# Cutting GpSimd's two runs of 16 products into pieces of four heads, with small mask products and a new order of the third stage

## The reference

```python
# L1_attn (letter D): 16 heads of 16 channels, 4 key heads, rope, a sink per head
att = einsum('bhqd,bhkd->bhqk', q, k) * hd ** (-0.5) + sink
att = softmax(where(band, att, -inf));  out = einsum('bhqk,bhkd->bqhd', att, v) @ wo
# L1_xattn (letter E): inside one token, 16 heads against 16 heads
Q, K, V = (x @ Wq.T + bq), (ctx @ Wk.T + bk), (ctx @ Wv.T + bv)   # as (token, 16, 16)
weight = softmax(einsum('bshd,bsgd->bshg', Q, K))
out = einsum('bshg,bsgd->bshd', weight, V) @ Wo.T + bo
# L1_ffn (letters F, M): causal attention, whose output goes only into a rank-16 modulation
mod = 0.1 * tanh(attn @ A)
gate = silu(h @ W_in.T + mod * (h @ A) @ B);  out = residual + gate * (h @ W_up.T) @ W_down.T
```

## Time and profile before

| | us |
|---|---|
| median of 3 runs | 3019.28 (3017.0 to 3025.15) |
| the profiled execution | 3016.38, span 3014.7 |
| first query product of the first tile | 1983.1 |
| last query product of the last tile | 2925.1 |

### The profile page before, as it was taken

One profiled execution on the slowest core, in us unless ns is written; L12 is line 12 of the kernel. 1 busy time (PEld: TensorE's weight loads), 2 busy tenths in 40 slices (PEclk: granted clock), 3 DMA queues, 4 the chain that ended last, 5 costly groups with the idle time before them and its releaser, 6 DMA issues. The chain is left out here.

```text
span 3014.7 us, 68300 instructions
## 1 busy us (share of the span) xinstructions
PE 2755.2 (91%) x22096; PEld 2297.8 (76%) x22128; DVE 2487.1 (83%) x5468; ACT 1990.4 (66%) x4233; POOL 2099.5 (70%) x2618
## 2 busy tenths in 40 slices
PE   6999999999999999999799499667899999999988
PEld 3888888888888888888555399535777777777767
DVE  6888888888888888888599677468889898989873
ACT  5888878878787887878576355345566666666642
POOL 6897666666666666666467544379898988898870
PEclk9999999999999999999899699768999999999999
DMA  4555444444434444444344499500000000000000
GB/s 145 176 197 167 134 138 139 146 139 131 143 132 141 139 146 140 132 153 132 116 155 158 173 333 341 191 15 19 20 24 23 24 22 24 22 24 23 21 4 11
DMA packets 185883, 340.11 MB, mean 113 GB/s; under 512 B 40668, under 2 KB 104037, under 8 KB 178936
## 3 DMA queue, kind: packets, MB, share of 16 engines
q1 hardware_dynamic: 179448, 319.55, 32.1%
q0 software_dynamic: 6144, 16.79, 1.7%
HBM read 264.68 MB, written 63.19 MB: 109 GB/s over the span
## 5 line engine op out<-in xcount | busy, mean ns | idle before, releaser
L1843 POOL TENSOR_TENSOR l_prod<-l_sco,l_kv 128x256 f32<-128x256 f32 x512 | 370.1, 762 | 35.4 <-DVE l_sco L2350 35.4
L1836 POOL TENSOR_TENSOR l_prod<-l_q,l_kv 128x256 f32<-128x256 f32 x512 | 359.2, 741 | 45.7 <-DVE l_att L2358 45.7
L718 DVE SCALAR_TENSOR_TENSOR a_cq<-a_PQ,a_taps,a_cq 128x504 f32<-128x504 f32 (+2 forms) x384 | 281.9, 734 | 74.9 <-ACT a_cq L584 65.8
L718 DVE SCALAR_TENSOR_TENSOR a_ck<-a_PK,a_taps,a_ck 128x504 f32<-128x504 f32 (+2 forms) x384 | 280.8, 731 | 9.4 <-ACT a_ck L584 0.3
L342 POOL TENSOR_TENSOR a_tq<-a_cq,a_tq 128x512 f32<-128x512 f32 x128 | 166.0, 1297 | 130.7 <-ACT a_tq L590 130.3
L329 POOL TENSOR_TENSOR a_hrs<-a_hve,a_neghalf 128x8 f32<-128x8 f32 x128 | 209.7, 1638 | 25.3 <-DVE a_hve L735 25.3
L485 PE MATMUL a_Y<-a_wo,a_og_parts 128*128 128x256 f32 x1536 | 207.2, 285 | 4.5 <-POOL a_og_parts L336 4.5
L412 PEld LDWEIGHTS a_X<-a_wv,a_xb 128*128 128x128 f32 x1536 | 199.8, 188 | 12.1 <-issue 1.2
L412 PE MATMUL a_PQ<-a_x_hi,a_wqk 128*128 (+1 forms) x512 | 196.1, 424 | 12.6 <-issue 11.9
L342 POOL TENSOR_TENSOR a_tk<-a_ck,a_tk 128x512 f32<-128x512 f32 x128 | 163.6, 1278 | 62.8 <-ACT a_tk L590 62.8
L412 PE MATMUL a_X<-a_wv,a_xb 128*128 128x256 f32 x1536 | 204.1, 282 | 0.8 <-DMA a_xb<-a_x_lo 0.8
(11 more groups left out here) (403 smaller groups left out, 8412.4 us busy)
## 6 DMA issues: line engine op xcount, KB each, us to landing
a_wqk<-qk_parts SPq DMA_DIRECT2D x112, 512.0 KB, 3.3
m_wgu<-gate_up_parts SPq DMA_DIRECT2D x39, 1024.0 KB, 7.9
a_wv<-v_parts SPq DMA_DIRECT2D x56, 512.0 KB, 3.7
a_wg<-g_parts SPq DMA_DIRECT2D x112, 256.0 KB, 3.1
a_wo<-o_parts SPq DMA_DIRECT2D x112, 256.0 KB, 2.8
a_dr<-decays SPq DMA_DIRECT2D x256, 64.0 KB, 2.5
m_hs<-sorted_rows SPq DMA_DIRECT2D x39, 256.0 KB, 7.1
sorted_outs<-m_ys SPq DMA_DIRECT2D x39, 256.0 KB, 7.3
```

The costliest lines, as they stand in the source:

```text
L718: nc.vector.scalar_tensor_tensor(out=acc, in0=src, scalar=taps[p][:, tap + k:tap + k + 1], in1=acc, op0=ALU.mult, op1=ALU.add).then_inc(s_ ...
L1836: nc.gpsimd.tensor_tensor(out=prod[:, h], in0=qv[:, h:h + 1, :].to_broadcast([P, H, HD]), in1=kk, op=ALU.mult).then_inc(S("E_pqk"), 1)
L1843: nc.gpsimd.tensor_tensor(out=prod[:, h], in0=sco[:, h:h + 1, :].to_broadcast([P, HD, H]), in1=vv, op=ALU.mult).then_inc(S("E_pav"), 1)
```

## The change

It has five parts.

1. GpSimd's products are cut into pieces of four heads. `q` and `sco` exist twice. Within an iteration, the first four heads of the next tile's queries come ahead of this tile's values; the values go in the order heads 4 to 15, then 0 to 3; heads 4 to 15 of the next tile's queries follow. Each piece waits for its own group of `prod`. VectorE's list follows: the scores of group 0 belong to the next tile, and the values of group 0 come last.
2. The gathers read the row numbers in `slots` directly; `of_tile` and the tiny instructions go.
3. The mask and sink products become four products of 64x512 each, one for each quarter of the array (`rows` by `s`).
4. `ft_gm` writes its result back into PSUM (`MI`), and `ft_gm_hi` and `ft_gm_lo` read it there.
5. The lists of all engines have a new order.

```diff
-        kv, q = [sb(f"kv{k}", [P, 2, D]) for k in range(3)], sb("q", [P, D])
+        kv, q = [sb(f"kv{k}", [P, 2, D]) for k in range(3)], [sb(f"q{k}", [P, D]) for k in range(2)]
-        sco, se = sb("sco", [P, H, H]), sb("se", [P, 3, H])
+        sco, se = [sb(f"sco{k}", [P, H, H]) for k in range(2)], sb("se", [P, 3, H])
...
-            def products_qk(t):
-                pool.wait_ge(S("E_q"), t + 1)
-                wait_if(pool, S("E_att"), 4 * t)
-                for h in range(H):
+            def products_qk(part):
+                def piece(t):
+                    pool.wait_ge(S("E_q"), t + 1)
+                    for h in range(4 * part, 4 * part + 4):
+                        if part == 0 and h == 0 and t >= 2:
+                            pool.wait_ge(S("E_att"), 4 * t - 4)
+                        if part and t and h % 4 == 0:
+                            pool.wait_ge(S("E_att"), 4 * t - 4 + h // 4)
...
+            def products_av(part):
+                def piece(t):
+                    pool.wait_ge(S("E_w"), t + 1)
+                    if part == 0:
+                        pool.wait_ge(S("E_sc0"), min(t + 2, TILES))
...
-                nc.gpsimd.tensor_copy(of_tile[:], slots[:, tile(t), :].rearrange("p t k -> p (t k)")).then_inc(S("G_at"), 1)
...
-                for half in range(2):
-                    if k == "F":
-                        nc.tensor.matmul(SS[:, half, :], identb[:], cmask[:], start=True, stop=False, skip_group_check=True)
-                    else:
-                        nc.tensor.matmul(SS[:, half, :], inverse3[:], sink3[:, half, :], start=True, stop=False, skip_group_check=True)
+                for s in range(2):
+                    for half in range(2):
+                        out = SS[s * SEQ:(s + 1) * SEQ, half, :]
+                        if k == "F":
+                            rows = slice(half * SEQ, (half + 1) * SEQ)
+                            nc.tensor.matmul(out, identb[rows, rows], cmask[rows], start=True, stop=False, skip_group_check=True)
+                        else:
+                            rows = slice(half * SEQ, half * SEQ + 3)
+                            nc.tensor.matmul(out, inverse3[rows], sink3[rows], start=True, stop=False, skip_group_check=True)
...
-                nc.vector.tensor_tensor(out=part[64:64 + R, :], in0=gmT[:], in1=part[0:R, :].bitcast(F32), op=ALU.subtract).then_inc(S("F_gm3"), 1)
+                nc.vector.tensor_tensor(out=part[64:64 + R, :], in0=MI[0:R, P:2 * P], in1=part[0:R, :].bitcast(F32), op=ALU.subtract).then_inc(S("F_gm3"), 1)
...
-            iterate(pool, [("F", power("F", 2)), ("Et", products_av), ("Dn", power("D", 1)), ("En", power("E", 1)), ("E", products_qk),
+            iterate(pool, [("F", power("F", 2)), ("E", products_qk(0)), ("Et", products_av(1)), ("Et", products_av(2)), ("Et", products_av(3)),
```

More of the change, by code:

```diff
@@ L1839, in products_av @@
[L1839 to L1849, removed]
-                nc.gpsimd.tensor_copy(of_tile[:], slots[:, tile(t), :].rearrange("p t k -> p (t k)")).then_inc(S("G_at"), 1)
[L1851 to L1854, removed]
+            def products_qk(part):
+                def piece(t):
+                    pool.wait_ge(S("E_q"), t + 1)
+                    pool.wait_ge(S(f"kv_in{t % 3}"), 16 * (t // 3 + 1))
+                    qv = q[t % 2][:].rearrange("p (h d) -> p h d", d=HD)
+                    kk = kv[t % 3][:, 0, :].rearrange("p (g d) -> p g d", d=HD)
+                    for h in range(4 * part, 4 * part + 4):
[3 more added lines that the diff above has]
+                            pool.wait_ge(S("E_att"), 4 * t - 4 + h // 4)
+                        nc.gpsimd.tensor_tensor(out=prod[:, h], in0=qv[:, h:h + 1, :].to_broadcast([P, H, HD]), in1=kk,
+                                                op=ALU.mult).then_inc(S("E_pqk1" if part else "E_pqk0"), 1)
+                return piece
@@ new lines, in products_av @@
+            def products_av(part):
[3 more added lines that the diff above has]
+                        pool.wait_ge(S("E_sc0"), min(t + 2, TILES))
+                    vv = kv[t % 3][:, 1, :].rearrange("p (d g) -> p d g", d=HD)
+                    for h in range(4 * part, 4 * part + 4):
+                        nc.gpsimd.tensor_tensor(out=prod[:, h], in0=sco[t % 2][:, h:h + 1, :].to_broadcast([P, HD, H]), in1=vv,
+                                                op=ALU.mult).then_inc(S("E_pav"), 1)
+                return piece
@@ L1855, in gather, with piece @@
+            def gather(k):
+                def piece(t):
+                    if t:
+                        pool.wait_ge(S("G_x"), 2 * t - 1 + k)
                     nc.gpsimd.indirect_dma_start(got[k][:], None, outs[:, :],
-                                                 bass.IndirectOffsetOnAxis(ap=of_tile[:, k:k + 1], axis=0)).then_inc(S(f"G_in{k}"), 16)
+                                                 bass.IndirectOffsetOnAxis(ap=slots[:, t, k:k + 1], axis=0)).then_inc(S(f"G_in{k}"), 16)
+                return piece
@@ L1858, in _ @@
             pool.wait_ge(S("masked"), 4)
-            iterate(pool, [("F", power("F", 2)), ("Et", products_av), ("Dn", power("D", 1)), ("En", power("E", 1)), ("E", products_qk),
-                           ("G", gather)])
+            iterate(pool, [("F", power("F", 2)), ("E", products_qk(0)), ("Et", products_av(1)), ("Et", products_av(2)), ("Et", products_av(3)),
+                           ("Et", products_av(0)), ("E", products_qk(1)), ("E", products_qk(2)), ("Dn", power("D", 1)), ("En", power("E", 1)),
+                           ("E", products_qk(3)), ("G", gather(0)), ("G", gather(1))])
@@ L2116, in e_q @@
             def e_q(t):
-                wait_if(act, S("E_pqk"), H * t)
+                if t >= 2:
+                    act.wait_ge(S("E_pqk1"), 12 * (t - 1))
                 act.wait_ge(S("E_qp"), t + 1)
-                nc.scalar.activation(q[:], EB[:, 0:D], ACT.Copy).then_inc(S("E_q"), 1)
+                nc.scalar.activation(q[t % 2][:], EB[:, 0:D], ACT.Copy).then_inc(S("E_q"), 1)
             def exponentials(k):
@@ L2222, in et_exp @@
                 act.wait_ge(S("E_sub"), t + 1)
-                nc.scalar.activation(sco[:], sco[:], ACT.Exp).then_inc(S("E_exp"), 1)
+                nc.scalar.activation(sco[t % 2][:], sco[t % 2][:], ACT.Exp).then_inc(S("E_exp"), 1)
             def split_high(t):
```

85 lines of the change are left out of this document (40 added, 45 removed).

## The result

The changed kernel takes 3122.23 us (median of 4 runs, 3097.49 to 3125.05) against 3018.14 for the kernel before: 1.0335 times as long, interval 1.0282 to 1.0388. It is slower; 2979 was forecast, and the range ended at 3014. The profiled execution is its quickest run, 3097.49, with a span of 3095.6 against 3014.7 before.

A forecast was written before the change was run, and what follows sets the result against it. TensorE, VectorE and GpSimd were all taken as nearly full. Iterations fall from 30.02 to 28.7 us: 36 us over 27, plus 4 in the ramp, so 2979 us on the runs' median; range 2953 to 3014.

The forecast's parts named there:

- VectorE (b): VectorE's cost of new overlap with GpSimd: weights 0.3 us, shift and low part of F 0.2 together, per iteration.
- GpSimd's stop for the last value sum: GpSimd's 1.25 us wait per iteration for VectorE's last value sum, from sharing `prod`; forecast to go.
- Small products: TensorE's four mask or sink products run side by side, 0.33 us instead of 0.53, saving 0.2 per stage.
- The 0.62: TensorE's 0.62 us wait before the output product, for ScalarE's copy of the transposed result; forecast to stay.
- all three engines were within two microseconds of full: TensorE, VectorE and GpSimd nearly full per iteration, so removing GpSimd's stops gains only what the next engine has left.
- VectorE and TensorE level: VectorE at 28.6 and TensorE at 28.65 us per iteration, waiting for each other; a little lost, giving 28.7.
- the 0.31 of the modulation's low part: VectorE's low part of the modulation: 283 ns instead of 592, with GpSimd idle and one operand in PSUM.
- The ramp: The four iterations before the steady part, 30.3 us each at a low clock; 1 us each gained, 4 together.
- Contention: Rival: weights, shift and low part of F all slow down, VectorE needs 29.2 us per iteration; 2993 us, chance 0.15.
- The slower case: Rival: each small mask or sink product on TensorE costs its whole 379 to 388 ns; 3046 us, chance 0.10.
- a new stop of over 1 us on PE: Sign of a wrong forecast: a new wait over 1 us on TensorE or VectorE inside the iteration.
- the two places that I thought likeliest: Likeliest new stops: the transpose of F behind the power, and the query projection behind ScalarE's copy.

The follow-up runs named there:

- E1: Changed kernel with the low part of F's input moved ahead of the first value sum, beside GpSimd's value products: 2968.35 us, ratio 0.985.
- E7: E1 with the mask and sink products of the kernel before, two of 128x512 per stage instead of four: 2960.69 us, ratio 0.9816.
- E8: E1 with the scaled modulation in SBUF, as in the kernel before, instead of PSUM: 2973.7 us, ratio 0.9839.
- E2: Kernel before with the low part of F's input moved behind the arguments of D, beside its 16 query products: 3018.11 us, ratio 0.9999.
- E6: Kernel before with the low part of F's input right behind a value sum, beside value products: 3016.7 us, ratio 0.9992.
- E14: E2 with four one-element tensor_scalar instructions ahead of the low part of F's input, to delay it: 3016.34 us, ratio 0.9984.
- E5: Changed kernel with the modulation's scaling put between the value sum and the low part of F's input: 3117.45 us, ratio 1.0328.
- E13: Changed kernel with eight one-element tensor_scalar instructions ahead of the low part of F's input, to delay it: 3130.49 us, ratio 1.037.
- E3: Changed kernel with GpSimd's power of D moved between the second and third groups of query products: 3029.18 us, ratio 1.0021.
- E9: Changed kernel with six one-element memsets ahead of the low part of F's input, to delay it: 3058.9 us, ratio 1.0123.
- E12: E1 with three tiny GpSimd instructions ahead of the first query piece, to shift the weights' moment: 2965.39 us, ratio 0.9803.
- E15: E1 with six one-element tensor_scalar instructions ahead of the low part of F's input, to delay it: 2986.85 us, ratio 0.9894.
- E4: Changed kernel with GpSimd waiting, before each query product of heads 5 to 15, for the previous one's end: 2974.14 us, ratio 0.9854.

## Why the prediction was wrong

**The step that failed** is VectorE (b): "the low part of F (412 at best, 895 at worst) up to 0.5 more". Its bounds came from rows in which the subtraction ran at other moments, and the change puts it behind the third of the four value sums, beside eight query products in a row. There it costs 4.9 us more in most tiles, ten times the upper bound. I had looked up what the weights and the shift would run beside, and not asked it of this instruction. With the one term replaced the sum comes near: 122.9 us more, less 40, is 83, and the span grew by 80.9. There is luck in that. GpSimd's value products, with first and last start, before and after:

```profile
L1843 POOL TENSOR_TENSOR l_prod<-l_sco,l_kv x512: 708/729/987, 1998.0 to 2940.3; 128x256 f32<-128x256 f32 x171
L1854 POOL TENSOR_TENSOR l_prod<-l_sco,l_kv x512: 707/731/995, 1990.9 to 3022.7; 128x256 f32<-128x256 f32 x171
```

From first to last they take 89.5 us more, and they begin 7.1 us earlier, which the forecast had left as it was. A held tile also costs more than the hold: at 34.1 us it is 6.1 longer than one of the same kernel in which the subtraction got in, and 5.4 longer than E1's, for a subtraction 4.8 and 4.7 longer. The granted clock (0.61 behind each wait) is part of that round, not a cause of its own: without the hold it is 1.00.

**The other terms held in the main.** E1 is the changed kernel without this term, and it takes 28.66 per tile for a forecast of 28.7, 2968 for 2979. That this comes out so close is in part luck: in E1 the weights cost 0.58 more and the subtraction 0.28, where 0.3 was taken for the one and 0.2 for the other and the shift together. GpSimd's stop for the last value sum is gone; that for the weights is gone in the changed kernel and 0.37 in E1, for 0.85 before. Apart from these it waits for the power of F, 1.59 in E1 where 1.4 was left for it. Weights: 0.65 in the changed kernel for a forecast 0.7, but 1.01 in E1. Small products: four of the sinks lie within 0.34 for a forecast 0.33, four of the mask within 0.22 in E1. The 0.62 stays. My remark that all three engines were within two microseconds of full was right for TensorE only: over that round VectorE was idle for 2.8 us and GpSimd for 3.0. E7 then speaks for VectorE alone setting the pace, not VectorE and TensorE level, so that what the small products save TensorE was no part of the gain. E8 shows that the 0.31 of the modulation's low part was right in size, but came mostly of the order, not of PSUM.

**The ramp** gained less than the 1 us each that I took. GpSimd's value products in the ramp of the changed kernel:

```profile
1990.86 11.31 POOL L1854 TENSOR_TENSOR l_prod<-l_sco,l_kv 128x256 f32<-128x256 f32 x16
...
2109.71 11.39 POOL L1854 TENSOR_TENSOR l_prod<-l_sco,l_kv 128x256 f32<-128x256 f32 x16
```

These four rounds take 118.9 us; before, from 1998.05 to 2119.52, the same four took 121.5, so 0.7 each is gained. The first is even longer than before (34.4 for 32.9). In the other three the subtraction got in, and they take 28.1 each for 29.5.

**The rivals.** Contention was priced at 1.1 us per tile in all, by the longest rows of before; it was the right mechanism with a price over four times too low. The slower case was looked for on TensorE, where four products did lie side by side. Of the signs named, "a new stop of over 1 us on PE" is what came, at the transpose of the value sums and not at the two places that I thought likeliest. The Trainium skill, SBUF — State Buffer, "SBUF: two separate sides", calls the pair that VectorE and GpSimd share an exclusive lock: who starts first has it for the whole instruction, and the other "fully blocks". The trace agrees for one product: in E2, E6 and E14 the subtraction gets in as the product under way ends. By that alone it could wait no longer than one product, 0.7 us. That the waiting instruction isn't next in line, and seven more products run ahead of it behind the one under way, is what the changed kernel's 5.35 us adds.

**Still open** is what lets it in. It is held beside query products (the changed kernel, E5, E13) and in some of the first and last tiles beside value products (the changed kernel, E3, E5, E7 to E9, E12, E13, E15); it gets in beside query products (E2, E14) and value products (E1, E6). All 17 traces together, 32 tiles each, leave no middle. In 28 tiles the subtraction found no product under way. In 351 it got in at the end of the product under way, and in 25, where it had started at most 0.11 us ahead of that end, at the next. In the other 140 it was held until GpSimd's products broke off, for another instruction (E3) or a wait (E4).

## What to carry to other kernels

When a change reorders an engine, list for each of VectorE's instructions with two SBUF inputs what GpSimd runs beside it afterwards, and bound its cost by the whole unbroken run of GpSimd instructions, not by the slowest row seen elsewhere. Such an instruction belongs beside a run that waits now and then, or where GpSimd does something else, or should read one operand from PSUM where it can (the low part of the modulation in E3 and E8), and work that an engine waits for shouldn't stand behind it. When a change of five parts loses, move back the one instruction whose row grew before judging the rest: here that alone turned 1.034 into 0.985.

## What the runs showed of the hardware

An instruction of 0.41 us on VectorE was held for 5.35 us, and 9.87 at most, by GpSimd products of 0.7 us each; started 0.05 us later (E9) it was not held in 10 tiles of 24. When it got in, it took the rest of the product under way and 0.28 us more (E1: some 0.42 and 0.28). An instruction that does get in lengthens the product beside it instead: in E1 the next product takes some 0.92 us for 0.72. A subtraction of 16x128 with one operand in PSUM was never held: at most 283 ns in E3, 25 of 32 times in the midst of a product. Other mask and sink products on TensorE changed VectorE's weights from 1.01 to 0.73 us (E7), and three tiny instructions on GpSimd from a median of 1.03 to 0.80 (E12): in each they start at another moment beside the products (0.05 us ahead of a product's end in E1, 0.44 in E7, 0.51 in E12). One-element memsets cost VectorE 0.01 us each behind a long sum, one-element `tensor_scalar` instructions about 0.06.
